# Setup of a long-convolution and feed-forward kernel: layers in quarters, another order of work, stores awaited in the next stage

## The chip, the cores and the metric

The kernel runs on one core of a Trainium2 chip. The metric is the time of one execution on the device, in microseconds (us). A core has TensorE (PE), VectorE (DVE), ScalarE (ACT), GpSimd (POOL) and SyncE (SP), each with its own instruction stream; SP here only issues DMAs and waits. The streams are ordered against each other by semaphores alone.

## The reference, cut to what matters

```python
xn = layernorm(x)                               # x: (4, 2048, 256)
# attention part: two orders of (long convolution, gate)
proj = xn @ in_proj_w + in_proj_b               # 256 -> 768
v = proj[..., :256]
for i in range(2):
    t = linspace(0, 1, 2048)
    ang = 2 * pi * freqs[i] * t
    enc = concat([sin(ang), cos(ang), t])       # 7 features
    h = gelu(enc @ w1[i] + b1[i])               # 64 wide
    h = gelu(h @ w2[i] + b2[i])
    h = (h @ w3[i] + b3[i]) * exp(-abs(decay[i]) * t * 2048)   # 2048 x 256
    v = fft_conv(v, h)
    xc = conv3(proj[..., (i+1)*256:(i+2)*256]) + conv_b[i]
    v = v * xc * sigmoid(xc @ gate_w[i] + gate_b[i])
a = v @ out_proj_w + out_proj_b
# feed-forward part, w_fc (1024 x 256) and w_proj (256 x 1024) made ternary
tern = clip(round(w / s), -1, 1),  s = mean(abs(w), axis=1)
f = relu(xn @ (tern_fc * s).T + gate * (xn @ v_.T @ fast_b.T @ u.T)) ** 2 @ (tern_proj * s_).T
out = x + a + f
```

## The kernel before

The program has three stages, each a block of five streams, with a barrier between two blocks. **Setup** (`setup_stage`) computes from the weights what the others need. **Project** (`project_stage`) goes over 16 chunks of 512 tokens: layer norm, input projection, short convolution, gates. **Mix** (`mix_stage`) does the long convolutions as products with Toeplitz tiles that are read from the DRAM tensor `filters`, the feed-forward part and the output. Only setup and one line of project are touched.

Within a stage every stream is written out by hand, in a fixed order. In setup:

- **The filters.** VectorE makes the time row `t` and the angles, ScalarE their sine into `enc` (L327). TensorE computes layer 1 (L364), ScalarE the gelu over all 2048 columns (L336), TensorE layer 2 (L368), ScalarE its gelu, TensorE layer 3 (L381) as four tiles w = 0 to 3 of 128 channels by 2048 lags. ScalarE makes the windows (Exp, L330) into `hT`. `filter_tile(w)` on VectorE multiplies the tile with its window (L281) and reduces the absolute values of two ranges of lags to `peaks`, the middle one of 128 and the far one of 1663 columns (L286). SP stores each tile to `filters`. At the end the peaks are transposed (L404) and reduced to the integers `flag`, which tell the mix stage how far each filter reaches; a peak counts when it isn't zero.
- **The ternary weights.** `ternary` on VectorE makes `fc_tern` and `pr_tern` from `fc_nat` and `pr_nat` (row means L253, comparisons L258 and L261). TensorE transposes them (L389, L395), ScalarE copies the results out (L348, L350), SP stores them as `fc_t` and `proj_t`. The scales of `w_proj` become a row by way of `diag` (L298, L400).
- **The low-rank part.** M1 is the small product of `v` and `fast_b` (L357); it waits for the four rank loads (`us`, `vs`, `fbT`, `gcol`). `ustack` holds u divided by the fc scales, is transposed (L372) and stored as `u_t`; `vrank` is stored as `v_t`.
- **Projection weights.** `Win` and `Wgate` are split in a high part (ScalarE) and the rest (VectorE, L293, L294).
- **x.** `statistics` on VectorE (L431, L434) and `rstd` and `normalise` on GpSimd prepare the first chunk of tokens.

SP issues all loads in one order, and at the end of setup waits for all 13 counted stores (L54 is the block's end). The project stage's first work on TensorE is the transposition of the first chunk (L795). V and GC1 of the later stages lie over setup's buffers: `hT`, `fc_nat` and the others are parts of V (written first at L651), `t`, `enc`, `h1`, `h2` and `projT` parts of GC1.

## Time and profile before

| | us |
|---|---|
| median of 3 runs | 929.61 |
| the three runs | 923.80, 929.61, 930.54 |
| profiled execution, its own time | 922.28 |
| its span, first to last instruction | 920.4 |
| PE busy | 838.2 (91%) |
| DVE busy | 632.2 (69%) |
| ACT busy | 467.5 (51%) |
| POOL busy | 242.6 (26%) |

The profiled execution is a fourth one beside the three timed runs. Its granted TensorE clock was 0.977 in the mean. Shares are over the whole span; the stages differ much in what they wait for.

### The profile page before, as it was taken

The page shows a single profiled execution, that of the slowest core. Times are in us where ns is not written, and L with a number is a line of the kernel's source. Part 1 is how long each engine was busy: PE and PEld are TensorE (multiplying, and loading weights), DVE is VectorE, ACT ScalarE, POOL GpSimd, SP SyncE. Part 2 cuts the span into 40 slices and gives each one's busy share as a digit, 9 for nine tenths or more (in the row PEclk, how much of TensorE's full clock was granted, in tenths as well). Part 3 has the DMA queues.
Part 4 walks back from the last instruction along what each step waited for, and adds up shares of the span by engine and source line. Part 5 has one row for each costly group of instructions (what it writes and reads, how often), then busy time and mean ns, then how long its engine had stood idle before and what let it go on. Part 6 is the DMA issues. An engine that isn't in the chain of part 4 may idle for free.

```text
span 920.4 us, 25865 instructions
## 1 busy us (share of the span) xinstructions
PE 838.2 (91%) x9894; PEld 699.6 (76%) x9895; DVE 632.2 (69%) x1041; ACT 467.5 (51%) x678; POOL 242.6 (26%) x259
## 2 busy tenths in 40 slices
PE   3837999999999994899999999999999999999995
PEld 1325888888888883678888888788877888788995
DVE  6963799899899885455556555665655556666884
ACT  6422777777777874344444344444434444443221
POOL 1023564664664610201111121210112011210111
PEclk9977999999999998999999999999999999999998
DMA  5363223324324217776787878867787867962893
GB/s 176 116 210 131 100 92 136 138 91 147 127 91 159 93 70 205 188 166 138 167 191 158 174 150 188 188 156 175 140 193 170 184 127 165 202 112 69 232 333 124
DMA packets 84390, 142.02 MB, mean 154 GB/s; under 512 B 12837, under 2 KB 62390, under 8 KB 83318
## 3 DMA queue, kind: packets, MB, share of 16 engines
q1 hardware_dynamic: 73734, 102.79, 47.3%
q0 software_dynamic: 10320, 37.49, 12.7%
q10 hardware_dynamic: 288, 1.11, 0.4%
q8 instruction: 29, 0.48, 0.2%
q14 instruction: 19, 0.16, 0.1%
HBM read 97.39 MB, written 43.97 MB: 154 GB/s over the span
## 4 chain that ended last, share of the span: by engine, by line
PE 43%; DMA 8%; DVE 5%; issue 2%; ACT 1%; SPq 1%; POOL 0%; DVEq 0%; ACTq 0%; POOLq 0%
PE py L1262 12%; PE pp L1243 11%; PE pf L1215 10%; DMA lead<-filters 7%; PE pf L1221 2%; PE py L1299 2%; PE py L1230 2%; DVE r_lo L1060 1%; PE pp L417 1%; PE pp L419 1%; PE pp L418 1%; DVE r L1055 1%; DVE pp L1045 1%; DMA srow<-scales 1%; DVE xb L1050 1%
## 5 line engine op out<-in xcount | busy, mean ns | idle before, releaser
L1262 PEld LDWEIGHTS py<-vwin,lead 64*64 64x64 f32 x5120 | 133.4, 133 | 33.1 <-issue 33.1
L1262 PE MATMUL py<-vwin,lead 64*64 64x128 f32 (+4 forms) x5120 | 147.2, 265 | 8.1 <-DMA lead<-filters 7.4
L1161 ACT ACTIVATE r_hi<-r 128x512 fp32r<-128x512 f32 x128 | 80.9, 632 | 142.9 <-DVE r L1055 142.9
L1060 DVE TENSOR_TENSOR r_lo<-r,r_hi 128x512 fp32r<-128x512 f32 x128 | 103.3, 807 | 67.1 <-ACT r_hi L1161 67.0
L1156 ACT ACTIVATE r<-pf,fscale 128x512 f32<-128x512 f32 x128 | 88.0, 687 | 117.1 <-PE pf L1221 116.9
L1243 PE MATMUL pp<-wproj,r_hi 128*128 128x256 f32 x512 | 134.7, 296 | 8.3 <-DVE r_lo L1060 3.1
L1215 PE MATMUL pf<-tokens,split_a 128*128 (+1 forms) x512 | 139.5, 394 | 0.5 <-issue 0.5
L1243 PE MATMUL pp<-wproj,r_lo 128*128 128x256 f32 x512 | 126.8, 281 | 0.0
L458 POOL TENSOR_SCALAR lead<-lead,norms 128x256 f32<-128x256 f32 x64 | 114.0, 1792 | 3.4 <-POOL norms L452 3.4
L1243 PEld LDWEIGHTS pp<-wproj,r_hi 128*128 128x128 f32 x512 | 96.2, 188 | 21.3 <-issue 6.3
L618 DVE SCALAR_TENSOR_TENSOR xc<-ctrl,taps,xc 128x512 f32<-128x512 f32 x128 | 97.2, 779 | 18.8 <-ACT xc L690 18.1
L1243 PEld LDWEIGHTS pp<-wproj,r_lo 128*128 128x128 f32 x512 | 96.3, 188 | 3.8 <-issue 1.8
L1215 PEld LDWEIGHTS pf<-tokens,split_a 128*128 128x128 f32 x512 | 87.3, 188 | 12.4 <-issue 0.8
L1055 DVE TENSOR_TENSOR r<-r 128x512 f32<-128x512 f32 x128 | 93.4, 730 | 2.0 <-ACT r L1156 1.8
L1399 POOL DMA_DIRECT2D tokens<-xnT_hbm x32 | 17.7, 555 | 180.6 <-PE pf L1221 146.6
L1100 DVE TENSOR_TENSOR V<-py,GC 128x512 f32 (+1 forms) x32 | 22.1, 691 | 61.5 <-PE pp L1243 59.6
L1102 DVE COPY V<-py 128x512 f32 (+1 forms) x32 | 22.1, 691 | 59.4 <-PE pp L1243 59.4
L417 PE MATMUL pc<-tokens,wgate_hi 128*128 128x512 f32 x128 | 54.5, 426 | 7.4 <-DVE tokens L624 7.3
L770 PEld LDWEIGHTS pn<-lead,xnT 128*64 128x64 f32 x1024 | 55.6, 137 | 5.6 <-issue 5.6
L417 PE MATMUL pc<-split_b,split_a 128*128 128x512 f32 x128 | 53.5, 418 | 6.9 <-DVE split_b L662 6.9
L770 PE MATMUL pn<-lead,xnT 128*64 128x128 f32 x1024 | 59.4, 274 | 0.0
L690 ACT ACTIVATE xc<-ctrl,taps 128x512 f32<-128x512 f32 x64 | 51.9, 811 | 13.5 <-DVE ctrl L612 10.3
(175 smaller groups left out, 1535.2 us busy)
## 6 DMA issues: line engine op xcount, KB each, us to landing
lead<-filters SPq DMA_DIRECT2D x128, 320.0 KB, 6.2
xnT_hbm<-split_b SPq DMA_DIRECT2D x32, 512.0 KB, 3.2
tokens<-xnT_hbm POOLq DMA_DIRECT2D x32, 512.0 KB, 7.4
lead<-in_attn_x SPq DMA_DIRECT2D x16, 512.0 KB, 3.9
gc_hbm<-xc SPq DMA_DIRECT2D x16, 512.0 KB, 2.6
GC<-gc_hbm SPq DMA_DIRECT2D x32, 256.0 KB, 7.1
out<-GC POOLq DMA_DIRECT2D x16, 512.0 KB, 5.8
GC<-in_attn_x POOLq DMA_DIRECT2D x9, 512.0 KB, 11.1
```

The costliest lines, as they stand in the source:

```text
L417: pe.matmul(out, w[0], x[0], start=start, stop=False, **more)
L458: last = pool.tensor_scalar(buf[:, i, :], buf[:, i, :], mv[:, i, 0:1], rs[:, i:i + 1], ALU.subtract, ALU.mult)
L618: dve.scalar_tensor_tensor(out=mixed(c), in0=tapped(ctrl[1 - par], c, k_), scalar=kw[:, c, k_:k_ + 1], in1=mixed(c), op0=ALU.mult, op1=ALU ...
L690: act.activation(mixed(c), tapped(ctrl[1 - par], c, 0), ACT.Identity, bias=kb[:, c:c + 1], scale=kw[:, c, 0:1]).then_inc(tap0_done, 1)
L770: last = pe.matmul(pn[side * BW:(side + 1) * BW, i, :].rearrange("p (h c) -> p h c", h=KT), xnT[:, k, ts], Wv_sides[:, k, :, side, :], sta ...
L1055: dve.tensor_tensor(r[j][:, :], r[j][:, :], r[j][:, :], ALU.mult).then_inc(sq_done, 1)
L1060: dve.tensor_tensor(r_lo[j][:, :], r[j][:, :], r_hi[j][:, :].bitcast(F32), ALU.subtract).then_inc(r_split, 1)
L1156: act.activation(r[j][:, :], pf[:, j, :], ACT.Relu, scale=fscale[:, m:m + 1]).then_inc(relu_done, 1)
L1161: act.activation(r_hi[j][:, :], r[j][:, :], ACT.Copy).then_inc(r_hi_done, 1)
L1215: last = pe.matmul(pf[:, m % 2, :], tern[:, k, ws], tokens(even, part, k), start=(k == part == 0), stop=False)
L1243: last = pe.matmul(pp[:, i, :], part[m % 2][:, i * P:(i + 1) * P], wproj[:, m, :], start=(m == 0 and n == 0 and i % 2 == 0), stop=(m == HT ...
L1262: last = pe.matmul(py[g % 2][q * BW:(q + 1) * BW, side, l, :, A:NB], tile[rows, q * PAIR + l, j * BW:(j + 1) * BW], vwin[g % 2][rows, q, l ...
```

## The change

- **Loads.** ScalarE's queue issues `fc_nat`, `vs`, `fbT`, `gcol`, `pr_nat`, `us` first of all; SP issues the loads of the layers, then x, then the rest. Four semaphores (frequencies, layer 1, other layers, each matrix) take the place of coarser ones.
- **Front.** VectorE makes `t` in one instruction, the angles in two halves, ScalarE the sine in two halves. TensorE multiplies two products of `ones` with a buffer of zeros (`warm`) ahead of M1 and two behind it. `enc` and `w1s` get 128 rows, with zeros in the new ones, which GpSimd and VectorE write.
- **Layers** 1 and 2 and their gelus go by quarters of 512 columns, each with its own count. All four windows come behind the gelus.
- **VectorE's order:** thresholds and ternary matrix of fc, statistics of x, tiles 0 and 1, `ustack`, tiles 2 and 3, thresholds of `w_proj`, `diag`, its ternary matrix, scale row, peaks. `filter_tile` reduces only the middle range; ScalarE sums the absolute values of the far one (`far_sum`). GpSimd makes the low parts of `Win` and `Wgate`.
- **Stores.** Setup's SP waits for four small stores alone (pads, `v_t`, `scales`). The other nine are waited for by VectorE in the first step of the project stage, in front of its write to V.

```diff
--- before.py
+++ after.py
...
+        enc = Gf[:, 2 * L:3 * L]
...
+        w1s = sb("w1s", [P, ORDERS * FO])
...
-            load(us[:, :, :], u.rearrange("(m p) r -> p m r", p=P), rank_in)
-            load(vs[:, :], v, rank_in)
-            load(fbT[:, :], fast_b.rearrange("i j -> j i"), rank_in)
-            load(gcol[:, :], bass.AP(gate.tensor, 0, [[0, P], [1, 1]]), rank_in)
...
-            load(fc_nat, w_fc.rearrange("(m p) d -> p m d", p=P), tern_in)
-            load(pr_nat, w_proj.rearrange("(k p) h -> p k h", p=P), tern_in)
...
+            load_x(sp)
...
-            load_first(sp)
+            load_taps(sp)
...
+            sp.wait_ge(ustack_ready, 2)
+            load(v_t, vrank[:, :, :, :].bitcast(F32), small_stored)
+            sp.wait_ge(ternT_ready, 1)
+            load(fc_t, tern.bitcast(F32), stored)
+            sp.wait_ge(srow_ready, 1)
+            load(scales, srow[0:1, :], small_stored)
             sp.wait_ge(ranks_ready, 1)
             load(u_t, ranks.bitcast(F32), stored)
-            sp.wait_ge(ustack_ready, 2)
-            load(v_t, vrank[:, :, :, :].bitcast(F32), stored)
-            sp.wait_ge(ternT_ready, 1)
-            load(fc_t, tern.bitcast(F32), stored)
             sp.wait_ge(proj_ready, 1)
             load(proj_t, projT.rearrange("p (m d) -> p m d", m=HT), stored)
-            sp.wait_ge(srow_ready, 1)
-            load(scales, srow[0:1, :], stored)
-            sp.wait_ge(stored, 16 * 13)
+            sp.wait_ge(small_stored, 16 * 4)
             sp.wait_ge(proj_in, 16 * PROJ_LOADS)
...
             normalise(pool, 0, 0)
+            pool.wait_ge(hi_ready, 1)
+            pool.tensor_tensor(Win[1][:, :, :], win_f[:, :, :], Win[0][:, :, :].bitcast(F32), ALU.subtract)
+            pool.wait_ge(hi_ready, 2)
+            pool.tensor_tensor(Wgate[1][:, :, :], gw_f[:, :, :], Wgate[0][:, :, :].bitcast(F32), ALU.subtract)
...
+            dve.memset(ones[:, :], 1.0).then_inc(warm_ready, 1)
+            dve.memset(warm, 0.0).then_inc(warm_ready, 1)
...
+            for h in range(2):
+                cols = slice(h * L // 2, (h + 1) * L // 2)
+                link(dve.tensor_scalar(rnd[:, cols], turns[:, cols], ROUND, None, ALU.add))
+                dve.scalar_tensor_tensor(out=turns[:, cols], in0=rnd[:, cols], scalar=ROUND, in1=turns[:, cols],
+                                         op0=ALU.subtract, op1=ALU.subtract).then_inc(angle_ready, 1)
...
-                for i, (first, end) in enumerate(((MID_FROM, FAR_FROM), (FAR_FROM, L))):
-                    part = hT[:, w, L - end:L - first] if w < KT else hT[:, w, first:end]
-                    dve.tensor_reduce(peaks[:, i, w:w + 1], part, AX.X, ALU.max, apply_absolute_value=True).then_inc(peak_ready, 1)
-
-            ternary(pr_nat, pr_tern, psc, pth, KT, HID).then_inc(tern_ready, 1)
+                part = hT[:, w, L - FAR_FROM:L - MID_FROM] if w < KT else hT[:, w, MID_FROM:FAR_FROM]
+                dve.tensor_reduce(peaks[:, 0, w:w + 1], part, AX.X, ALU.max, apply_absolute_value=True).then_inc(peak_ready, 1)
+
+            dve.wait_ge(fc_in, 16)
+            thresholds(fc_nat, fsc, fth, HT, D)
+            ternary(fc_nat, fc_tern, fth, HT)
+            statistics(dve, 0, 0, True)
...
-            dve.wait_ge(hi_ready, 2)
-            dve.tensor_tensor(Win[1][:, :, :], win_f[:, :, :], Win[0][:, :, :].bitcast(F32), ALU.subtract)
-            dve.tensor_tensor(Wgate[1][:, :, :], gw_f[:, :, :], Wgate[0][:, :, :].bitcast(F32), ALU.subtract)
...
             filter_tile(2)
+            filter_tile(3)
+            dve.wait_ge(down_in, 16)
+            thresholds(pr_nat, psc, pth, KT, HID)
...
-            filter_tile(3)
-
-            statistics(dve, 0, 0, True)
-
+            ternary(pr_nat, pr_tern, pth, KT)
...
+            act.dma_start(fc_nat, w_fc.rearrange("(m p) d -> p m d", p=P)).then_inc(fc_in, 16)
+            act.dma_start(vs[:, :], v).then_inc(rank_in, 16)
+            act.dma_start(fbT[:, :], fast_b.rearrange("i j -> j i")).then_inc(rank_in, 16)
+            act.dma_start(gcol[:, :], bass.AP(gate.tensor, 0, [[0, P], [1, 1]])).then_inc(rank_in, 16)
+            act.dma_start(pr_nat, w_proj.rearrange("(k p) h -> p k h", p=P)).then_inc(down_in, 16)
+            act.dma_start(us[:, :, :], u.rearrange("(m p) r -> p m r", p=P)).then_inc(rank_in, 16)
...
+                act.wait_ge(angle_ready, h + 1)
+                act.activation(enc[0:TIME_ROW, cols], enc[0:TIME_ROW, cols], ACT.Sin, scale=-TWO_PI).then_inc(enc_ready, 1)
...
+            for j in range(4):
+                act.wait_ge(l1_mm, j + 1)
+                act.activation(h1[:, j * 512:j * 512 + 512], ps[:, j, :], ACT.Gelu, bias=b1s[:, :]).then_inc(h1_ready, 1)
+            for j in range(4):
+                act.wait_ge(l2_mm, j + 1)
+                act.activation(h2[:, j * 512:j * 512 + 512], ps[:, j, :], ACT.Gelu, bias=b2s[:, :]).then_inc(h2_ready, 1)
+
+            act.wait_ge(ndec_ready, 1)
+            for w in range(4):
...
+                act.activation(junk[:, w, 0:L - FAR_FROM], part, ACT.Abs, accum_out=peaks[:, 1, w:w + 1]).then_inc(peak_ready, 1)
+
+            far_sum(0)
+            far_sum(1)
+            act.wait_ge(ternT_mm, 1)
+            act.activation(tern, upper, ACT.Copy).then_inc(ternT_ready, 1)
+            far_sum(2)
+            far_sum(3)
...
+            pe.wait_ge(warm_ready, 2)
+            for _ in range(2):
+                pe.matmul(ps[:, 7, :], ones[:, :], warm, start=True, stop=True)
             pe.wait_ge(rank_in, 16 * RANK_LOADS)
-            pe.wait_ge(ident_ready, 1)
...
+            for _ in range(2):
+                pe.matmul(ps[:, 7, :], ones[:, :], warm, start=True, stop=True)
+
+            pe.wait_ge(layer1_in, 16 * LAYER1_LOADS)
+            pe.wait_ge(t_row_ready, 1)
+            for j in range(4):
+                pe.wait_ge(enc_ready, j // 2 + 1)
+                pe.matmul(ps[:, j, :], w1s[:, :], enc[:, j * 512:j * 512 + 512], start=True, stop=True).then_inc(l1_mm, 1)
...
-            pe.wait_ge(h1_ready, 1)
-            for j in range(4):
-                last = pe.matmul(ps[:, j, :], w2s[:, :], h1[:, j * 512:j * 512 + 512], start=True, stop=True)
-            last.then_inc(l2_mm, 1)
-            pe.wait_ge(ustack_ready, 2)
-            for m in range(HT):
-                last = pe.transpose(upper[0:HALF, m * P:(m + 1) * P], ustack[:, m, :, :].bitcast(F32).rearrange("p s r -> p (s r)"), ident[:, :])
-            last.then_inc(uT_mm, 1)
-            pe.wait_ge(h2_ready, 1)
-            pe.wait_ge(ranks_ready, 1)
+                pe.wait_ge(h1_ready, j + 1)
+                pe.matmul(ps[:, j, :], w2s[:, :], h1[:, j * 512:j * 512 + 512], start=True, stop=True).then_inc(l2_mm, 1)
+            pe.wait_ge(ustack_ready, 1)
...
+                    if w == 0:
+                        pe.wait_ge(h2_ready, j + 1)
...
+            pe.wait_ge(ustack_ready, 2)
+            pe.wait_ge(ternT_ready, 1)
+            for m in range(HT):
+                last = pe.transpose(upper[0:HALF, m * P:(m + 1) * P], ustack[:, m, :, :].bitcast(F32).rearrange("p s r -> p (s r)"), ident[:, :])
+            last.then_inc(uT_mm, 1)
+            pe.wait_ge(diag_ready, 1)
+            pe.matmul(ps[:, 6, 0:D], ones[:, :], diag[:, :, :].rearrange("p k c -> p (k c)"), start=True, stop=True).then_inc(srow_mm, 1)
...
                     dve.wait_ge(v_mm, s + 1)
+                    if s0 == 0:
+                        dve.wait_ge(stored, 16 * STORES)
```

TensorE's order in setup, from its first product to layer 3 (GC1 holds `enc`, `h1` and `h2`; a row with x3 is three more of its kind). Before:

```order
L357 MATMUL ps_setup<-fbT,vs 128x16 [waits ident_ready,rank_in]
L364 MATMUL ps_setup<-GC1,w1s 128x512 [waits enc_ready,t_row_ready,filter_in]
L364 MATMUL ps_setup<-GC1,w1s 128x512 x3
L368 MATMUL ps_setup<-GC1,w2s 128x512 [waits h1_ready]
L368 MATMUL ps_setup<-GC1,w2s 128x512 x3
L372 MATMUL ps_setup<-ident,GC1 64x128 [waits ustack_ready]
L372 MATMUL ps_setup<-ident,GC1 64x128 x7
L381 MATMUL ps_setup<-GC1,w3s 128x512 [waits ranks_ready,h2_ready]
```

After (V is the part that holds `warm`):

```order
L380 MATMUL ps_setup<-V,ones 128x512 [waits warm_ready]
L383 MATMUL ps_setup<-fbT,vs 128x16 [waits rank_in]
L386 MATMUL ps_setup<-V,ones 128x512 x2
L392 MATMUL ps_setup<-GC1,w1s 128x512 [waits enc_ready,t_row_ready,layer1_in]
L392 MATMUL ps_setup<-GC1,w1s 128x512 [waits enc_ready] x3
L396 MATMUL ps_setup<-GC1,w2s 128x512 [waits h1_ready,filter_in]
L396 MATMUL ps_setup<-GC1,w2s 128x512 [waits h1_ready] x3
L405 MATMUL ps_setup<-GC1,w3s 128x512 [waits h2_ready,ustack_ready]
L405 MATMUL ps_setup<-GC1,w3s 128x512 [waits h2_ready] x3
```

Four products are new, every quarter waits for its own input, and the transposes of `ustack` (L372) have left this place.

VectorE's order from the first filter tile to the scale row. Before:

```order
L281 SCALAR_TENSOR_TENSOR V<-ps_setup,b3s,V 128x2048 [waits l3_mm,win_ready]
L286 TENSOR_REDUCE peaks<-V 128x1 [waits h_ready]
L286 TENSOR_REDUCE peaks<-V 128x1
L293 TENSOR_TENSOR split_a<-win_f,split_a 128x1024 [waits hi_ready]
L294 TENSOR_TENSOR wgate_lo<-gw_f,wgate_hi 128x1024
L298 TENSOR_SCALAR diag<-ident,psc 128x128 [waits ident_ready]
L431 BN_STATS norms<-lead 128x6 [waits x_loaded0]
L305 TENSOR_TENSOR peaks<-peaks 128x4 [waits peak_ready]
L307 COPY scale_row<-ps_setup 128x256 [waits srow_mm]
```

After, from the last filter tile on:

```order
L283 SCALAR_TENSOR_TENSOR V<-ps_setup,b3s,V 128x2048 [waits l3_mm,win_ready]
L287 TENSOR_REDUCE peaks<-V 128x1 [waits h_ready]
L273 TENSOR_REDUCE psc<-V 128x2 [waits down_nat_in]
L306 TENSOR_SCALAR diag<-ident,psc 128x128 [waits ident_ready,dve_step]
L265 TENSOR_SCALAR V<-V,pth 128x1024 x2
L268 SCALAR_TENSOR_TENSOR V<-V,pth 128x1024 [waits dve_step]
L311 COPY scale_row<-ps_setup 128x256 [waits srow_mm]
L313 TENSOR_TENSOR peaks<-peaks 128x4 [waits peak_ready]
```

The second ternary matrix (its reduction L273, comparisons L265 and L268) stands behind the tiles instead of ahead of them; the statistics and the low parts are gone from there.

## Rows read from the trace of the kernel before

**Rows 1.** windows view: us, busy us of PE, PEld, DVE, ACT, POOL; clock, DMA, GB/s

```profile
0.00:67.90 67.90, 35.98 (x102) 18.03 (x103) 51.24 (x84) 29.13 (x20) 10.35 (x20) 0.93 0.57 170
```

**Rows 2.** the waits of SP's queue, 0 to 110 us; total, times, longest

```profile
SPq L54 <- DMA scales<-scale_row: 4.9, 1, 4.9
```

**Rows 3.** the block end L54, 60 to 70 us; duration min/median/max in ns

```profile
L54 POOLq DRAIN  x1: 4837/4837/4837, 61.3 to 61.3; - x1
```

**Rows 4.** timeline of TensorE, 0 to 110 us; start, us, what, [idle before]

```profile
6.67 1.03 PE L357 MATMUL ps_setup<-fbT,vs 16*128 16x16 f32 x4 [6.67 <-DMA gcol<-in_ffn_gate]
14.52 7.16 PE L364 MATMUL ps_setup<-GC,w1s 65*128 65x512 f32 x8 [6.82 <-ACT GC L327]
23.74 5.80 PE L368 MATMUL ps_setup<-GC,w2s 128*128 128x512 f32 x8 [2.06 <-ACT GC L336]
...
32.59 14.25 PE L381 MATMUL ps_setup<-GC,w3s 128*128 128x512 f32 x32 [2.18 <-ACT tokens L343]
...
54.65 3.03 PE L395 MATMUL ps_setup<-ident,V 128*128 128x128 f32 x16 [2.89 <-DVE V L281]
...
58.35 1.21 PE L404 MATMUL ps_setup<-ident,peaks 128*1 128x128 f32 x8
67.98 1.94 PE L795 MATMUL pT<-ident,lead 128*128 128x128 f32 x8 [8.42 <-PEq L54]
```

**Rows 5.** timeline of TensorE's weight loads, 21 to 31 us

```profile
27.32 0.34 PEld L368 LDWEIGHTS ps_setup<-GC,w2s 128*128 128x128 f32 x1 [0.52 <-issue]
28.09 0.19 PEld L368 LDWEIGHTS ps_setup<-GC,w2s 128*128 128x128 f32 x1 [0.44 <-issue]
```

**Rows 6.** timeline of ScalarE, 0 to 110 us

```profile
14.39 1.28 ACT L330 ACT_TABLE_LOAD   x1
15.69 3.89 ACT L330 ACTIVATE V<-GC,ndec 128x2048 f32<-128x2048 f32 x2
...
21.72 1.97 ACT L336 ACTIVATE GC<-ps_setup,b1s 128x2048 f32<-128x2048 f32 x1 [0.84 <-PE ps_setup L364]
```

**Rows 7.** timeline of VectorE, 0 to 110 us

```profile
19.09 2.29 DVE L253 TENSOR_REDUCE fscale<-V 128x8 f32<-128x2048 f32 x1 [6.17 <-DMA V<-in_ffn_w_proj]
...
28.68 2.27 DVE L253 TENSOR_REDUCE psc<-V 128x2 f32<-128x2048 f32 x1
...
32.91 2.48 DVE L261 SCALAR_TENSOR_TENSOR V<-V,pth 128x1024 f32<-128x1024 f32 x2
36.37 2.35 DVE L281 SCALAR_TENSOR_TENSOR V<-ps_setup,b3s,V 128x2048 f32<-128x2048 f32 x1 [0.98 <-PE ps_setup L381]
...
51.77 0.47 DVE L298 TENSOR_SCALAR diag<-ident,psc 128x128 f32<-128x128 f32 x2
52.15 2.35 DVE L281 SCALAR_TENSOR_TENSOR V<-ps_setup,b3s,V 128x2048 f32<-128x2048 f32 x1
...
59.60 0.68 DVE L310 TENSOR_REDUCE reach<-ps_setup 1x1 f32<-1x512 f32 x1 [0.61 <-PE ps_setup L404]
...
61.85 0.18 DVE L316 CAST flag<-reach 1x65 int32<-1x65 f32 x1
...
85.49 1.23 DVE L651 TENSOR_TENSOR V<-pn,bv_row 128x1024 f32<-128x1024 f32 x1 [2.84 <-PE pn L770]
```

**Rows 8.** VectorE's groups by line and form, 19 to 62 us

```profile
L286 DVE TENSOR_REDUCE peaks<-V 128x1 f32<-128x1663 f32 x4 | 7.5, 1874 | 0.0
```

**Rows 9.** timeline of SP's queue, 0 to 110 us

```profile
10.43 0.59 SPq L137 DMA_DIRECT2D V<-in_ffn_w_fc  x1
...
61.45 0.81 SPq L137 DMA_DIRECT2D scales<-scale_row  x1
```

**Rows 10.** DMA issues, 0 to 75 us; KB each, median us to landing

```profile
V<-in_ffn_w_proj SPq DMA_DIRECT2D x1, 1024.0 KB, 8.0
...
us<-in_ffn_u SPq DMA_DIRECT2D x1, 64.0 KB, 2.3
```

**Rows 11.** GpSimd's groups by line and form, whole span

```profile
L984 POOL TENSOR_TENSOR xb<-xb,bo_row 128x1024 f32<-128x1024 f32 x7 | 17.8, 2536 | 45.3 <-DMA xb<-in_attn_x 45.3
```

149 lines of the change are left out of this document (71 added, 78 removed).

## Prediction

> **What bounds the kernel now.** I read the views in this order. The windows view puts the whole setup stage into 0 to 67.9 us [rows 1]. In it TensorE works 36.0 us of 67.9, VectorE 51.2, ScalarE 29.1: no engine is full, so setup is a chain that changes engines, and the change touches nothing else. Behind it the project and mix stages stay as they are; they start from a barrier, so setup's end moves them as a block, and what counts is when TensorE's first product of the project stage (L795) starts, now at 67.98 [rows 4].
>
> Three things end late. VectorE writes the flags until 62.03 (61.85 + 0.18) [rows 7]. GpSimd, which gets the statistics of x last, leaves its drain at 66.1 (61.3 + 4.84) [rows 3]. SP issues the last store at 61.45, is free at 62.26 and waits 4.9 us for the stores to land, until 67.16 [rows 2, 9]; TensorE starts 0.8 us later.
>
> The chain to 62.03, backwards [rows 4, 7]: the last filter tile is multiplied by VectorE from 52.15; the four tiles start at 36.37, when L381 has filled the first banks. L381 (layer 3) starts at 32.59, and is ready for it only because layer 1 starts at 14.52 (waiting for the sine), layer 2 at 23.74 and each gelu takes a whole 2048 columns (1.97 us, [rows 6]) between layers. VectorE's own load is the other strand: it waits for both weight matrices until 19.09, and makes both ternary matrices before tile 0.
>
> **The change part by part.** Times are on the clock of the profiled execution.
>
> *TensorE's front.* Layer 1 will be behind the small product M1 and two pairs of products of zeros. The trace counts each full fp32 product as two passes: eight for four products. At the lower clock a pass costs 7.16/8 = 0.895 us, at the higher 14.25/32 = 0.445 [rows 4]. Pair one runs from about 2.5 to 6.1 while nothing else could. M1 waits for all four rank loads, and `us` is now last on ScalarE's queue, behind both weight matrices. Before, the two matrices took from 10.43 (issue) to 19.09 (VectorE starts on them), 8.6 us [rows 7, 9]. Issued from about 1.0 they are in at 9.7. `us` alone took 2.3 us from issue to landing [rows 10]; issued by 4, it is in the same queue right behind, so I add 0.8 us for its bytes: 10.5, with bounds of 8 (it does not wait for the matrices' ends) and 13 (SP's x loads take half of the engines from 8 us on). Before, M1 started at 6.67: this part of the change costs a wait. M1 takes 1.03 [rows 4], ends at 11.5; pair two, 4 x 0.895 = 3.6, ends at 15.1. So layer 1 starts 0.6 us *later* than now, at 15.1. The sine is no bound any more: it was ready at 14.52, and loses a conversion and one of VectorE's passes and is cut in halves.
>
> *The clock.* The eight passes of layer 1, with 65 rows, keep TensorE busy for 7.16 us at 0.895 each and the clock does not rise; the passes of layer 2, with 128 rows, start slow at 23.74 and the weight load at 28.09 is the first short one (0.19 instead of 0.34 us), 4.35 us later [rows 4, 5]. That is the step from 1.2 to 2.4 GHz. The change gives layer 1 128 rows and puts 128-row products ahead. Taking 4.35 us from 11.5, the clock is up at 15.9: layer 1 pays one slow pass and seven fast, 0.9 + 3.1, and ends at 19.1. Bounds: clock up already at 15.1 (0.4 us less), or only when layer 1 is done (7 x 0.45 = 3.2 us more).
> The Trainium skill ("TensorE: Matmul & The Clock Gate", Part 1) says that the default is the slow clock and sustained activity releases it. Layer 1's 7.16 busy us at the slow rate say that busy time alone is not enough here; by the page layer 1 would be fast from its first pass, 0.4 us less, by the row as summed.
>
> *Quarters.* Layer 2's pass over quarter j waits for gelu j alone. A quarter of a gelu is about 0.5 to 0.7 us (1.97 for four, [rows 6]), less than the 0.89 of a quarter's two passes, so TensorE runs through: layer 2 19.1 to 22.7, layer 3's first tile right behind. The present gaps of 2.06 and 2.18 us ahead of layers 2 and 3, and the eight transposes of `ustack` between them, are gone from there. Layer 3 keeps its 14.25 us [rows 4]: 22.7 to 37.0. The windows (Exp) now come after the gelus: last gelu at about 23.4, one table load of 1.28, 1.95 for each [rows 6]: the first at 26.6, tile 0's products at 26.3. So VectorE starts tile 0 at 26.7 instead of 36.37, and each tile (2.35 + a short reduction) is quicker than TensorE's 3.56 for the next. The long reductions of 1.87 us, four of them [rows 8], go to ScalarE, where there is room: windows until 32.5, two copies, four sums of about 1.6 (1663 columns at the gelu's rate), two more copies, some 44 in all, before the 46.9 below. VectorE reaches tile 0 with time left: it is held until M1's result at about 12.3, then comes the first ternary matrix, which with the `ustack` steps took from 19.09 to 28.68, 9.6 us [rows 7]; that leaves 4.8 us ahead of 26.7 for the four short statistics instructions.
>
> Tile 3 starts at **37.1 instead of 52.15: 15.0 us earlier**.
>
> *The tail gets longer.* The second ternary matrix moves behind tile 3. It took from 28.68 to 35.39 (32.91 + 2.48), 6.7 us, the diagonal 0.47 [rows 7]. 37.1 + 2.35 + 0.3 + 6.7 + 0.5 = 46.95. Only then can TensorE transpose it, 3.03 us at the low clock, and the peaks, 1.21 [rows 4]: 51.2. The flags' chain was 59.60 to 62.03, 2.4 us [rows 7]; with 0.2 of hand-over it ends at **53.8, 8.2 us earlier than 62.03**. The statistics of x are done by 26.7, so GpSimd normalises long before; the two low parts of weights that it takes over (about 2.5 us each by its nearest row, [rows 11]) end near 41.
>
> *The stores.* SP now waits only for four small ones. The 4.9 us go, and with them the 5.1 us from 62.03 to 67.16. Behind the tail nothing waits: barrier and start 0.8 us as before, 54.6. **67.98 - 54.6 = 13.4 us.** The wait is moved in front of VectorE's first write to V, which was at 85.49 [rows 7] and will be at 72.1. The last large store, issued at 46.95 + 3.0 + 1.9 (ScalarE's copy, a 2048-column instruction) + 0.5 = 52.4, lands some 5.7 us later (61.45 to 67.16 with two large ones in the queue [rows 2, 9]): 58.1, so 14 us of cover. Without this cover the 5.1 us would come back, no more.
> The Trainium skill ("DMA: Bandwidth & Descriptors", Issuing engines are not separate DMA queues) speaks against the second queue: transfers from all queues run on the same engines, and only issue time is saved. Here issue order is what held the matrices back (fc was issued at 10.43); by that rule the sharing with x puts M1 at the upper bound, 13, which gives a gain of 10.9 instead of 13.4.
>
> **From the gain to a time.** The profiled execution took 922.28 us with a span of 920.4; less 13.4 it is 908.9. It is the fastest of the four times known: the median of the runs is 929.61, less 13.4 it is 916.2. I take the middle of the four (923.8 and 929.61, mean 926.7): **913.3 us**, a ratio of 1.015. A measurement of this kernel can tell about 1% (9 us) from no change.
>
> **Rivals.**
> (a) *Late front.* `us` lands at 13, or the clock rises only behind layer 1. For: the queue is in order, and SP loads x at the same time. Against: the two matrices alone were done in 8.6 us. It costs 2.5 to 5.7 us: gain 7.7 to 10.9, time about 917.5. Chance 0.20, about half of it above 1%.
> (b) *The clock stays low: slower than before.* If products of zeros and the broken stream do not raise TensorE (7.16 us of layer 1 did not), every pass of the layers costs 0.45 us more: 7 + 8 + 32 passes, 21.2 us, against 13.4 gained: 7.8 us slower, 934.5. It decides from 30 slow passes on. Against: layer 2 rose after 4.35 us with 128 rows, and after 15.1 the new order has no gap. Chance 0.04.
> (c) *Early front.* `us` in at 8, clock up when layer 1 starts: 3 us more, gain 16 to 17, time 910. Chance 0.10.
> (d) *The tail is fuller than I see*, or the change does not remove the wait at the end: stores still queued hold one of SP's small ones (the scales are behind the transposed fc matrix). If SP again waits 5 us, gain 8.3: 918.4. Against: the scales are issued near 47.5, 6 us before VectorE's end. Chance 0.08, with other losses that leave under 1%, or a small loss, 0.06 more.
> The forecast itself, gain 11 to 16: 0.52.
>
> **Numbers.** Faster by over 1%: the forecast, (c), half of (a), a part of (d), some of it lost where runs scatter: 0.74. Slower by over 1%: 0.05. Within 1%: 0.21. The range takes the gains from 8 to 17 on the scatter of the base: 905 to 922.
>
> **What will show it.** In the changed profile: M1 near 10.5 and layer 1 near 15; short weight loads from about 16; L283's four tiles from 26.7 to 37; L55 without a DMA wait on SP; the first pT transposes at 54.6; V written near 72 without idle time put down to a store. If M1 starts much later than 10.5, step *TensorE's front* is wrong; if L392 to L405 have passes of 0.85, *the clock*; if L827 starts more than 1 us after VectorE's flag cast, *the stores*. The prediction fails as a whole if the project or mix stage changes its own length, 852.4 us from 67.98 to the end.

## Result and the profile after

The changed kernel takes 917.07 us (four runs, 913.4 to 923.1) against 927.83 us for the one before (four runs, 923.8 to 930.5): a ratio of 0.9876, 95% interval 0.984 to 0.9912, or 10.8 us. A second set on another occasion gave 915.54 us (six runs) against 927.22 us (eleven), again 0.9876 [0.9846, 0.9906], 11.7 us. The forecast was 913.3 us in a range of 905 to 922.

The profiled execution took 916.67 us, with a span of 915.1 us. TensorE's timeline in setup shows the start, the layers, the tail and the hand-over to the project stage, against [rows 4] (start, us, what, idle before it and its releaser):

```profile
2.68 3.78 PE L380 MATMUL ps_setup<-V,ones 128*128 128x512 f32 x4 [2.68 <-DVE V L234]
11.92 1.03 PE L383 MATMUL ps_setup<-fbT,vs 16*128 16x16 f32 x4 [5.46 <-DMA us<-in_ffn_u]
12.88 3.78 PE L386 MATMUL ps_setup<-V,ones 128*128 128x512 f32 x4
16.45 4.40 PE L392 MATMUL ps_setup<-GC,w1s 128*128 128x512 f32 x8
20.69 3.60 PE L396 MATMUL ps_setup<-GC,w2s 128*128 128x512 f32 x8
24.12 13.90 PE L405 MATMUL ps_setup<-GC,w3s 128*128 128x512 f32 x32
...
47.88 3.67 PE L427 MATMUL ps_setup<-ident,V 128*128 128x128 f32 x16 [2.62 <-DVE V L268]
51.34 1.46 PE L434 MATMUL ps_setup<-ident,peaks 128*1 128x128 f32 x8
55.88 1.94 PE L827 MATMUL pT<-ident,lead 128*128 128x128 f32 x8 [3.08 <-PEq L55]
```

The first transpose of the project stage is at 55.88 instead of 67.98 us: **setup is 12.1 us shorter**. This start is the measure of all setup experiments below. It is steadier than the time of a run, but not exact: two more profiles with this same setup have it at 55.71 and 54.59, and the kernel before has it at 67.98 and 68.31. So the gain of setup is 12.1 to 13.7 us by the pair that is compared, and a difference of 1.3 us or less at this point shows nothing by itself. The start of tile 3 on VectorE (38.13, 38.37 and 37.29 in the three) leaves the tail's part of this scatter out. Between layers 1, 2 and 3 there is no idle time in brackets any more, where [rows 4] had 2.06 and 2.18 us; on the other side stands a new wait of 5.46 us for `us`. The weight loads show the rise of the clock at 18.12, as [rows 5] do at 28.09:

```profile
17.31 0.34 PEld L392 LDWEIGHTS ps_setup<-GC,w1s 128*128 128x128 f32 x1 [0.52 <-issue]
18.12 0.19 PEld L392 LDWEIGHTS ps_setup<-GC,w1s 128*128 128x128 f32 x1 [0.47 <-issue]
```

VectorE's timeline, against [rows 7]: tile 0, tile 3, the ternary form of `w_proj` behind it, the flags, and the first write to V, which now follows the wait for the stores:

```profile
28.36 2.35 DVE L283 SCALAR_TENSOR_TENSOR V<-ps_setup,b3s,V 128x2048 f32<-128x2048 f32 x1 [4.08 <-ACT V L355]
...
38.13 2.35 DVE L283 SCALAR_TENSOR_TENSOR V<-ps_setup,b3s,V 128x2048 f32<-128x2048 f32 x1 [0.38 <-PE ps_setup L405]
...
40.72 2.27 DVE L273 TENSOR_REDUCE psc<-V 128x2 f32<-128x2048 f32 x1
...
45.34 2.48 DVE L268 SCALAR_TENSOR_TENSOR V<-V,pth 128x1024 f32<-128x1024 f32 x2
...
52.84 0.68 DVE L316 TENSOR_REDUCE reach<-ps_setup 1x1 f32<-1x512 f32 x1 [4.61 <-PE ps_setup L434]
...
55.09 0.18 DVE L322 CAST flag<-reach 1x65 int32<-1x65 f32 x1
...
72.80 1.22 DVE L683 TENSOR_TENSOR V<-pn,bv_row 128x1024 f32<-128x1024 f32 x1 [2.84 <-PE pn L802]
```

Two readings matter here. The flag cast ends at 55.27 and TensorE starts 0.6 us later, so no store is waited for at the end of setup. And V's first write waits 2.84 us for TensorE, to the hundredth what it waited before [rows 7]: the deferred wait for nine stores costs nothing there. SP's queue confirms the end: the last store is issued before VectorE is done, and of the 4.9 us wait for a DMA of [rows 2] there is nothing.

```profile
48.18 0.24 SPq L143 DMA_DIRECT2D scales<-scale_row  x1
48.46 0.48 SPq L143 DMA_DIRECT2D u_t<-tokens  x1
53.49 0.33 SPq L143 DMA_DIRECT2D proj_t<-GC  x1
```

From the first transpose to the end the two profiled executions differ the other way: 852.4 us before, 859.2 us after. That pair alone would say that half of the gain is handed back. The last part of the next section is about it.

### The profile page after: what moved, and what is told of

It reads as the page before. It is cut to its first block, busy times and chain, and to the rows that moved or that the text cites. A ratio compares the mean times of both kernels' runs of the same rounds, so it can differ in the third digit from the quotient of the medians.

```text
span 915.1 us, 25896 instructions
## 1 busy us (share of the span) xinstructions
PE 842.4 (92%) x9902; PEld 701.7 (77%) x9903; DVE 625.7 (68%) x1036; ACT 472.7 (52%) x692; POOL 247.6 (27%) x262
## 4 chain that ended last, share of the span: by engine, by line
PE 44%; DMA 6%; DVE 6%; issue 3%; ACT 1%; SPq 0%; DVEq 0%; POOL 0%; ACTq 0%; POOLq 0%
PE py L1294 12%; PE pp L1275 12%; PE pf L1247 10%; DMA lead<-filters 5%; PE pf L1253 2%; PE py L1331 2%; PE py L1262 2%; DVE r L1087 1%; DVE r_lo L1092 1%; DVE pp L1077 1%; PE pp L447 1%; PE pp L449 1%; PE pp L448 1%; DVE xb L1082 1%; DMA srow<-scales 1%
## 5 line engine op out<-in xcount | busy, mean ns | idle before, releaser
L1092 DVE TENSOR_TENSOR r_lo<-r,r_hi 128x512 fp32r<-128x512 f32 x128 | 105.5, 825 | 67.1 <-ACT r_hi L1193 67.0
L722 ACT ACTIVATE xc<-ctrl,taps 128x512 f32<-128x512 f32 x64 | 51.9, 811 | 13.7 <-DVE ctrl L642 10.5
## 6 DMA issues: line engine op xcount, KB each, us to landing
GC<-in_attn_x POOLq DMA_DIRECT2D x9, 512.0 KB, 11.9
```

Source lines behind the costliest of these rows:

```text
L722: act.activation(mixed(c), tapped(ctrl[1 - par], c, 0), ACT.Identity, bias=kb[:, c:c + 1], scale=kw[:, c, 0:1]).then_inc(tap0_done, 1)
L1092: dve.tensor_tensor(r_lo[j][:, :], r[j][:, :], r_hi[j][:, :].bitcast(F32), ALU.subtract).then_inc(r_split, 1)
```

## Experiments

Each starts from the changed kernel unless it says otherwise. Its own first transpose is compared with 55.88 us.

### The stores are waited for in setup again

```diff
             sp.wait_ge(small_stored, 16 * 4)
+            sp.wait_ge(stored, 16 * STORES)
```

> The changed kernel, but SyncE waits in setup for all 13 stores again, as before the change. Measured by the start of projection's first transpose in the profile (55.88 us in the changed kernel). Theory, from the profile of the changed kernel: proj_t is issued at 53.49 and has landed at about 57.4, VectorE's last instruction ends at 55.27, so the block would end 2.1 us later, and the first transpose stands at 58.0 to 58.5: the deferred stores were worth 2 to 2.5 us of the 12.1. Rival: SyncE is 4 to 5 us late, as in the kernel before, where its last wait ended beside a drain of GpSimd of 4.8 us: first transpose at 60 to 61.

First transpose at 58.63. The layers and tile 3 were 0.35 us late in this run (tile 3 at 38.48 against 38.13), which leaves 2.4 us; and from the end of the flag cast (55.78) to the first transpose it is 2.85 us instead of 0.61. So the deferred stores are worth 2.2 to 2.4 us. The waits of SP's queue name the one that is back:

```profile
SPq L143 <- ACT GC L375: 4.5, 1, 4.5
SPq L199 <- DMA proj_t<-GC: 3.5, 1, 3.5
```

The rival falls: not 5 us, since only one store is still under way when VectorE ends, and VectorE ends 2 us behind the issue of that store.

### TensorE without products of zeros, with 65 rows, and with neither

```diff
-            for _ in range(2):
-                pe.matmul(ps[:, 7, :], ones[:, :], warm, start=True, stop=True)
```
in both places for the first, for the second
```diff
-                pe.matmul(ps[:, j, :], w1s[:, :], enc[:, j * 512:j * 512 + 512], start=True, stop=True).then_inc(l1_mm, 1)
+                pe.matmul(ps[:, j, :], w1s[0:TIME_ROW + 1, :], enc[0:TIME_ROW + 1, j * 512:j * 512 + 512], start=True, stop=True).then_inc(l1_mm, 1)
```
and both edits for the third.

> The changed kernel without its four products of zeros (two ahead of M1, two behind it); layer 1 still runs over 128 rows. Theory: layer 1 then starts where the first sine ends (12.95 us, against 16.45), its first passes run slow and the clock rises some 4 to 5 us after it starts, at 17 to 18, as it does now; layer 1 ends at 19 to 20 (20.85 now), and tile 3 and the setup's end come 0 to 1.5 us earlier: the products of zeros cost what they give. Rival, the way the change is written: without them TensorE is at half clock through layer 2, the gelus of layer 2 end 1 us or more later than the 25.0 of now, and projection's first transpose comes 1 to 3 us later than 55.88.

> The changed kernel, but layer 1 multiplies 65 rows as before instead of 128 (63 of them zeros). Theory: the clock rises by the share of TensorE's rows in use, so the 65-row passes leave it low; all eight passes of layer 1 and the first of layer 2 are slow, with short weight loads (0.19 us) appearing only 2 us or more later than 18.12; the second gelus end 1 to 3 us later than 25.0, and the setup ends 1 to 3 us later. Rival: busy time alone raises the clock, whatever the rows: weight loads become short at 18.1 +- 0.4, and nothing moves by over 0.4 us.

> The changed kernel with no products of zeros and layer 1 over 65 rows: neither of the two edits that were to raise the clock. Without the zero products alone the clock rose 4.4 us after layer 1 began (128 rows, from 12.97), and layer 1 ended at 18.9; with 65 rows but the zero products it had risen at 16.35. Theory: in passes of 65 rows the clock does not rise, as in the kernel before (8 passes, 7.16 us, all slow): layer 1 ends at 19.8 to 20.2, layer 2 stays slow for 3 to 4 us, layer 3 begins 1 to 2.5 us later than in the run without zero products alone (21.76), and projection's first transpose comes at 55.5 to 57, against 54.58. Rival: the rows do not matter: clock up at 17.4, first transpose at 54.2 to 55.0.

| kernel | layer 1 starts | first short weight load | layer 1 takes | layer 3's first load | tile 3 starts | first transpose |
|---|---|---|---|---|---|---|
| changed | 16.45 | 18.12 | 4.40 | 23.70 | 38.13 | 55.88 |
| changed, second profile | 17.21 | 17.93 | 3.88 | 23.94 | 38.37 | 55.71 |
| changed setup in the run without bias, below | 16.42 | 16.42 | 3.60 | 22.86 | 37.29 | 54.59 |
| no zero products | 12.97 | 17.89 | 5.94 | 21.76 | 36.19 | 54.58 |
| 65 rows | 16.35 | 16.35 | 3.60 | 22.79 | 37.23 | 54.58 |
| neither | 13.94 | 23.41 | 7.20 | 25.13 | 39.56 | 57.53 |

The windows view cannot tell the level of the clock this early: it reads 1.00 for the eight slow passes of before (14.52 to 21.70), because the trace's first record of the clock is its rise, at 28.0. Ahead of that, the length of a pass tells it: 0.90 us at the low clock, 0.45 at the high one.

Without the zero products tile 3 starts 1.1 to 2.2 us *earlier* than in the three profiles of the changed setup (1.1 to 2.1 with M1 at the same time): layer 1 waits for the second pair, and without it the clock rises during layer 1 itself. At the first transpose only 0.0 to 1.3 us of this are seen, since VectorE waited longer for the peaks (5.07 us against 4.15 to 4.61). With 65 rows alone nothing is lost, against my theory: the clock had risen at the end of the second pair, and all eight 65-row passes behind it are fast. It rose early in this run, 3.4 us after that pair began instead of 5.2. That is no work of the edit, and neither are the 1.3 us of this row: the run without bias has the changed setup with all 128 rows, and shows the same early rise and the same end, to 0.1 us:

```profile
16.42 3.60 PE L392 MATMUL ps_setup<-GC,w1s 128*128 128x512 f32 x8
...
54.59 1.94 PE L827 MATMUL pT<-ident,lead 128*128 128x128 f32 x8 [3.08 <-PEq L55]
```

What passes over 65 rows did in no profile is raise the clock from the low level. That shows where neither edit is there:

```profile
13.94 7.20 PE L388 MATMUL ps_setup<-GC,w1s 65*128 65x512 f32 x8
20.93 4.79 PE L392 MATMUL ps_setup<-GC,w2s 128*128 128x512 f32 x8
```

All eight passes of layer 1 are slow again, 7.20 us as in [rows 4] (7.16), without a gap, and weight loads get short at 23.41, 3.3 us after those of layer 2 with 128 rows began (20.08). In this run `us` landed about 1 us late; less that, tile 3 would be at about 38.6 and the first transpose at about 56.6. So, without zero products, 128 rows in layer 1 are worth some 2.4 us at tile 3 and 2.0 at the first transpose (each from one profile). At tile 3 the zero products take back 1.1 to 2.1 of these 2.4, and the clock part of the change nets 0.3 to 1.3 us.

### The load of `us` first

```diff
+            act.dma_start(us[:, :, :], u.rearrange("(m p) r -> p m r", p=P)).then_inc(rank_in, 16)
             act.dma_start(fc_nat, w_fc.rearrange("(m p) d -> p m d", p=P)).then_inc(fc_in, 16)
...
-            act.dma_start(us[:, :, :], u.rearrange("(m p) r -> p m r", p=P)).then_inc(rank_in, 16)
```

> The changed kernel, but the load of u (the fourth that M1 waits for) is issued first on ScalarE's queue instead of behind both weight matrices; M1 waited 5.46 us for it. Theory: M1 runs at 7 to 8.5 us instead of 11.9; the second pair of zero products follows it and is over before the sine (12.05); layer 1 starts at 12.1 to 13.0 instead of 16.45 and the tiles and the end of setup come 1.5 to 4 us earlier. If TensorE falls idle between the zero products and the sine, layer 1 runs slow for 4 to 5 us from its start and the gain is nearer 1.5. Rival: M1 is late for another load (v, fast_b or the gate, all issued on the same queue), then nothing moves by over 0.5 us.

First transpose at 51.64: **3.0 to 4.2 us earlier** than in the three profiles of the changed setup (tile 3, at 34.35, 2.9 to 4.0 us), the largest gain that a single edit added to the changed kernel. Its timeline:

```profile
9.02 0.61 PE L383 MATMUL ps_setup<-fbT,vs 16*128 16x16 f32 x4 [2.56 <-DMA gcol<-in_ffn_gate]
9.56 3.46 PE L386 MATMUL ps_setup<-V,ones 128*128 128x512 f32 x4
12.82 3.86 PE L392 MATMUL ps_setup<-GC,w1s 128*128 128x512 f32 x8
```

`us` lands 2.4 us after its issue, not 7.8; what is now late is the gate, which is still issued behind the first matrix, so M1 comes at 9.02 and not at 7 to 8.5. The clock rises in the first passes of layer 1 (weight loads of 0.19 us from 13.51), and VectorE goes from the statistics into tile 0 at 24.70 without its wait of 4.08 us.

### The ternary form of `w_proj` ahead of tile 0

```diff
             statistics(dve, 0, 0, True)
+            dve.wait_ge(down_in, 16)
+            thresholds(pr_nat, psc, pth, KT, HID)
+            ternary(pr_nat, pr_tern, pth, KT)
             filter_tile(0)
```
(and out from behind tile 3)

> The changed kernel, but VectorE makes the ternary form of w_proj (8 instructions, 6.7 us) behind the statistics of x, ahead of tile 0, where it waited 4.08 us for ScalarE's window, and not behind tile 3. Theory: VectorE is 2.6 us late for tile 0 and the four tiles shift by that; behind tile 3 there are 6.7 us less of VectorE's work; projT's transposes then follow tile 3 directly, and projection's first transpose comes 3.5 to 4.5 us earlier than 55.88, at 51.4 to 52.4. Rival: the tail is bound by TensorE and ScalarE (transposes, the copies of tern and ranks), and the shift of 2.6 us eats what is left: 0 to 1.5 us earlier, or later.

First transpose at 55.36: 0.5 us earlier than 55.88 and 0.8 later than 54.59, so no gain is shown, the rival's case. Tile 0 came at 30.69, as forecast, but the way to tile 2 grew, and the tail was bound elsewhere:

```profile
33.08 8.83 PE L405 MATMUL ps_setup<-GC,w3s 128*128 128x512 f32 x16 [2.69 <-DVE V L283]
42.02 1.94 PE L414 MATMUL ps_setup<-ident,V 128*128 128x128 f32 x16
46.02 1.13 PE L419 MATMUL ps_setup<-ident,GC 128*64 128x128 f32 x8 [2.06 <-ACT tokens L368]
```

TensorE's transposes of fc wait until VectorE has read tile 2 out of the same banks (41.87), and from there the chain is transposes, ScalarE's copy, transposes of `ustack`, transposes of projT, whoever made the ternary matrix. VectorE's copy of `ustack` stands in the way too, 2.47 us instead of 0.43; its row, and the one of GpSimd beside it:

```profile
36.82 2.47 DVE L301 CAST GC<-GC 128x512 fp32r<-128x512 f32 x1
```
```profile
36.60 2.40 POOL L219 TENSOR_TENSOR wgate_lo<-gw_f,wgate_hi 128x1024 fp32r<-128x1024 f32 x1
```

It ends (39.29) just behind GpSimd's two-input instruction (39.00), and in the changed kernel, where GpSimd's begins at 35.04, it runs ahead of it at 0.43.

### The far parts by VectorE again

```diff
                 dve.tensor_reduce(peaks[:, 0, w:w + 1], part, AX.X, ALU.max, apply_absolute_value=True).then_inc(peak_ready, 1)
+                far = hT[:, w, 0:L - FAR_FROM] if w < KT else hT[:, w, FAR_FROM:L]
+                dve.tensor_reduce(peaks[:, 1, w:w + 1], far, AX.X, ALU.max, apply_absolute_value=True).then_inc(peak_ready, 1)
...
-            far_sum(0)
-            far_sum(1)
...
-            far_sum(2)
-            far_sum(3)
```

> The changed kernel, but VectorE reduces the far part of each filter tile to its peak again (four reductions of 1663 elements, 1.87 us each) and ScalarE's four far sums are gone. Theory: VectorE is the busy engine from tile 0 to the end of w_proj's ternary form (waits of 0.23 and 0.38 us in 20 us), so nearly all of the 7.5 us comes back: projection's first transpose at 62 to 63.5 us instead of 55.88. Rival: the tail is bound by the transposes and ScalarE's copies as much as by VectorE, and only 2 to 4 us come back (58 to 60).

First transpose at 66.04, 10.2 us later; less 1.4 us for an M1 at 13.33, **8.8 us** (10.1 against the profile at 54.59), beyond the theory's 7.5 for the four instructions themselves. The rest are their followers: the same copy of `ustack` beside GpSimd (2.45 us), and TensorE, idle for 4.01 us ahead of the transposes, which then take 3.65 instead of 1.91 us, at the low clock:

```profile
44.16 3.65 PE L412 MATMUL ps_setup<-ident,V 128*128 128x128 f32 x16 [4.01 <-DVE V L283]
```

Of the parts tried, moving the far sums is worth most: without it the rest of the change would be worth some 3 us (67.98 against 64.6).

### Gelus in halves

```diff
-            for j in range(4):
-                act.wait_ge(l1_mm, j + 1)
-                act.activation(h1[:, j * 512:j * 512 + 512], ps[:, j, :], ACT.Gelu, bias=b1s[:, :]).then_inc(h1_ready, 1)
+            for j in range(2):
+                act.wait_ge(l1_mm, 2 * j + 2)
+                act.activation(h1[:, j * 1024:j * 1024 + 1024], lower[:, j * 1024:j * 1024 + 1024], ACT.Gelu, bias=b1s[:, :]).then_inc(h1_ready, 1)
```
and layer 2's alike.

> The changed kernel, but the gelus of both layers run in halves of 1024 columns (four ScalarE instructions instead of eight), and layers 2 and 3 wait for halves. Theory: quarters hide all of ScalarE's latency in TensorE's layers; with halves layer 2 starts where it does now or 0.3 us later, the last gelu of layer 2 ends 0.3 to 1.0 us later than 25.0, and all that follows is 0.3 to 1.5 us later than 55.88. Rival, the way the forecast counted it: with halves TensorE waits 2 us ahead of layer 2 and again ahead of layer 3, as in the kernel before, its clock falls, and the first transpose is 3 us or more later.

First transpose at 55.77. TensorE runs through the three layers all the same (16.63, 20.68, 24.12), since half a gelu (1.11 us) is shorter than the four passes it hides behind (1.72). Tile 0 came 0.4 us later and tile 3 0.3 us later than in the changed kernel; at the first transpose nothing of it can be told from the scatter. The rival falls: no wait and no slow clock come back with halves. That cutting the layers at all is what matters is read from [rows 4] (2.06 and 2.18 us of waiting ahead of layers 2 and 3, which are gone); no run has the changed kernel with uncut layers.

### GpSimd's additions in the mix stage

The profile after shows instructions of VectorE in the mix stage that take 1.8 to 2.9 us instead of 0.69, each beside an addition of GpSimd (a row of GpSimd's timeline, then one of VectorE's):

```profile
728.26 2.39 POOL L1016 TENSOR_TENSOR GC<-GC,bo_row 128x1024 f32 x1 [9.11 <-DMA GC<-in_attn_x]
```
```profile
728.49 2.70 DVE L1092 TENSOR_TENSOR r_lo<-r,r_hi 128x512 fp32r<-128x512 f32 x1 [0.70 <-ACT r_hi L1193]
```

GpSimd's ends at 730.65 and VectorE's half a microsecond later, at 731.19. What these instructions take beyond 0.69 us sums to 24.6 us after (14 of them) and to 20.9 before (13).

```diff
-                pool.tensor_tensor(buf, buf, bo_row[:, :].unsqueeze(1).broadcast_to([P, TT, D]), ALU.add).then_inc(xb_biased, 1)
+                pool.tensor_tensor(buf[:, 0, 0:1], buf[:, 0, 0:1], bo_row[:, 0:1], ALU.add).then_inc(xb_biased, 1)
```

> The changed kernel without the addition of out_proj's bias to x in the mix stage: GpSimd adds one element instead of 128x1024 (its output lacks that bias). In the changed kernel's profile 14 of GpSimd's 16 additions (2.4 us each) ran beside a two-input instruction of VectorE, which then took 2.1 to 2.9 us instead of 0.69, 24.6 us in all. Theory: with the additions gone no VectorE instruction of r or r_lo takes over 0.9 us there; TensorE waits less for r_lo, the kernel is 5 to 20 us shorter than 917, and its runs lie within 2 us of one another. Rival: the collisions lie beside TensorE's work: under 3 us, and the runs scatter as before by 7 us or more.

> The kernel before, with the same addition left out. Theory: without the collisions' scatter the two kernels differ by what setup gained less what is given back: 12.1 us less 2.5 us for GpSimd's drain at the start of mix (9.57 against 7.05 us), so this run is 9 to 12 us longer than the changed kernel without bias. Rival: the collisions themselves took part of the gain (their sum was 20.9 us before, 24.6 after), and then the difference grows to 12 to 14 us.

912.83 us (six runs, 909.7 to 919.1) and 924.01 us (twelve, 919.9 to 927.0), beside 928.18 us (seventeen, 921.7 to 932.1) for the kernel before. The hits are gone from both, which the group of L1092 of the changed kernel without bias shows (mean 689 ns, against 825 in the changed kernel):

```profile
L1092 DVE TENSOR_TENSOR r_lo<-r,r_hi 128x512 fp32r<-128x512 f32 x128 | 88.2, 689 | 67.1 <-ACT r_hi L1193 67.0
```

But 20.9 us of VectorE are worth only about 4 us of the kernel before (ratio 0.9963 [0.9941, 0.9985]) and 24.6 us only 3 to 4 of the changed one (between its two medians and 912.83), and the runs scatter over 7 to 9 us as before. The hits are real and mostly hidden; the scatter is not theirs. The two kernels differ by 11.2 us here, where their first transposes differ by 13.7 (68.31 and 54.59).

### Where the runs scatter, and a combined version

```diff
+            pe.wait_ge(ranks_ready, 1)
+            pe.wait_ge(peak_ready, 9)
+            for i in range(2):
+                for w in range(4):
+                    last = pe.transpose(ps[0:1, 4 + i, w * P:(w + 1) * P], peaks[:, i, w:w + 1], ident[:, :])
+            last.then_inc(peakT_mm, 1)
             pe.wait_ge(tern_ready, 2)
             pe.wait_ge(h_ready, 4)
```
The combined version has `us` first as well, and VectorE's maximum of the peaks stands between the two halves of the ternary form.

> The changed kernel with u's load issued first on ScalarE's queue, and with the transposes of the peaks (and VectorE's maximum ahead of them) moved in front of the transposes of projT, so that VectorE's reach chain of 2.4 us runs beside projT's copy. With u first alone the first transpose came at 51.64. Theory: the peaks are transposed at 42.0, VectorE ends at 46.9 and the end is set by ScalarE's copy of projT at 49.6 and the issue of its store: first transpose at 50.1 to 50.8, 5.1 to 5.8 us earlier than 55.88, and the median of runs 4 to 6 us under that of the changed kernel. Rival: VectorE waits for ScalarE's far sums inside the ternary form, projT comes later by that, and nothing is gained over 51.64.

> The changed kernel once more, unchanged, for a second profile and a time on the same chip as the combined version. Theory: first transpose at 55.3 to 56.8 (the load of u and the rise of the clock each scatter by half a microsecond or more), median 915 to 918; its time from there on is 855 to 862 us like that of the other runs, longer than the 852.4 of the profiled execution of the kernel before only because that one was 6 us faster than its median. Rival: the rest is always 857 or more after the change and the kernel before has 852, so that half of setup's gain is handed back; then the medians would differ by 6 us.

The combined version starts projecting at 50.20, 5.7 us earlier than the changed kernel's first profile and 4.4 earlier than its earliest. Its flags are cast by 46.48, and the end is now ScalarE's copy of projT (48.98) and the store's issue. Its median is 908.94 us (905.3 to 917.0), a ratio to the kernel before of 0.9805 [0.9765, 0.9845], 6.6 us under the changed kernel on the same chip.

The changed kernel once more has its first transpose at 55.71 and again 859.2 us from there on. Over all profiles that rest is 852.4 us (before) and 853.2 (before without bias); after, it is 854.7, 856.8, 857.9, 858.4, 858.9, 859.2, 859.2, 859.5, 860.8, 861.5, 861.6 and 866.8. The profiled execution of before is 5.9 us faster than the median of its 17 runs; a median run of it has a rest of 858.3 if its setup is the same, and a median run of the changed kernel has 858.1 to 859.6. From medians the setup's 12.1 us arrive as 10.8 and 11.7, so 0.4 to 1.3 us are given back, no more than these medians can tell; against a setup that is 13.7 us shorter it would be 2.0 to 2.9, and the kernels without bias say 2.5. Of the 6.8 us between the first two profiles 4.6 lie in the mix stage (from TensorE's first product there to the end 551.0 us before and 555.7 after; 552.0 before without bias, 551.4 to 564.0 over all profiles after). Both profiles of before have a shorter rest than all twelve after, though most of these are variants. Whether anything of this is real, and where it comes from, stays open. A candidate was the wait of TensorE at the block between project and mix, 6.4 us before and 8.9 after. It does not hold: the kernel before without bias has 8.2 there, and two changed variants 7.3 and 6.3.

A part of the scatter is one wait. At the start of the second order TensorE waits for a filter block; these are the rows of before, of the changed kernel, and of the version with halves, in that order:

```profile
681.05 2.28 PE L1262 MATMUL py<-vwin,lead 64*64 64x128 f32 x80 [1.89 <-DMA lead<-filters]
```
```profile
671.80 2.28 PE L1294 MATMUL py<-vwin,lead 64*64 64x128 f32 x80 [1.92 <-DMA lead<-filters]
```
```profile
677.65 4.28 PE L1294 MATMUL py<-vwin,lead 64*64 64x128 f32 x80 [4.09 <-DMA lead<-filters]
```

After a wait of 1.9 us the 80 products take 2.28 us, after 4.1 us (3.65 with `us` first) 4.28 us, and in the combined version 3.61 us after 2.88: the clock has fallen. At this place the wait is 1.9 to 4.1 us over the fourteen profiles. The four profiles after the change with 3.5 us or more have a rest of 862.0 us in the mean, the other eight one of 858.4; but these eight alone spread from 854.7 to 861.5, so most of the scatter has other causes, which were not looked for. The windows view of that iteration gives both costs together, 33.0 us at a granted clock of 1.00 (the changed kernel again) and 37.9 us at 0.91 (halves):

```profile
660.60:693.60 33.00, 30.76 (x526) 25.63 (x525) 18.15 (x25) 13.18 (x21) 4.64 (x4) 1.00 0.81 166
```
```profile
664.90:702.80 37.90, 33.55 (x526) 28.26 (x525) 16.15 (x25) 13.18 (x21) 4.72 (x4) 0.91 0.72 148
```

A wait that is 2.1 us longer goes with an iteration that is 4.9 us longer. What makes that block late in one run and not in another was not tried.

## Why the prediction was right, and where it was not

The outcome was the forecast's own case by setup's gain: 12.1 us where 13.4 were counted (11 to 16), none of the rivals (b), (c) or (d). The other pairs of profiles give 12.3 to 13.7. The gain in time, 10.8 us, would also fit rival (a), and its mechanism, a late front, is there at part of its price. By its steps:

- *TensorE's front*: M1 10.5 forecast, 11.92 measured (12.68 in the second profile); layer 1 15.1 against 16.45. In direction this was right, down to layer 1 starting later than before the change, and the 0.8 us by which `us` lands behind the matrices was too (1.0). The matrices were late: the sum carried the 8.6 us of before over to an issue at 1.0 and had them in at 9.7, and they landed at 10.85. So `us`, issued at 4.03 behind two loads of 1 MB, needed 7.8 us. This is rival (a)'s mechanism at half of its lower price (1.4 of 2.5 us), and moving one line removes it. What followed from the Trainium skill ("DMA: Bandwidth & Descriptors", Issuing engines are not separate DMA queues) was an M1 at 13, since loads of both queues share the engines; the measured 11.9 to 13.3 (over the ten profiles that kept this order of loads) lie nearer to that than my 10.5.
- *The clock*: rise forecast 4.35 us behind M1's end, at 15.9; it came at 18.12, 5.2 us behind. The same stretch was 4.9 (no zero products), 3.4 (65 rows) and 3.3 (neither), and the kernel before itself has 5.2 in its second profile (the one without bias), so the one row of before was no constant. Forecast was one slow pass in layer 1, there were about two, and layer 2 began at 20.69 and not at 19.1.
- *Quarters*: no gaps between the layers, right; layer 3 took 13.90 us. Tile 0 at 28.36 (forecast 26.7) and tile 3 at 38.13 (37.1): tile 0 waits for ScalarE's window, behind gelus that ended 1.6 us late, and tile 3 for TensorE, 1.4 us late at the start of layer 3 and 0.35 quicker in it. The cut's fineness did not count, as the halves show. Of the 14.0 us by which tile 3 comes earlier (52.15 to 38.13) 6.5 hang on the far parts' move to ScalarE (tile 3 at 46.04 without it, less 1.4 for its late M1), and 8.8 at the hand-over; the prediction did not price this move by itself.
- *The tail gets longer*: from tile 3 to the last flag 16.7 us forecast, 17.14 measured (38.13 to 55.27); the transposes of projT took 3.67 instead of 3.03. Right, and the early-ternary run shows why it could not simply be moved back.
- *The stores*: release 0.6 us (forecast 0.8), first V write at 72.80 (72.1) without a store's wait. Right. But the 4.9 us of [rows 2] were not all to be had from this edit: in the new order the wait is worth 2.2 to 2.4 us.
- *From the gain to a time*: the base of 926.7 was close to the medians of later sets (927.2 to 928.2). Of the miss of 3.8 us (917.07 against 913.3) 1.3 are setup's in the first pair of profiles; the other 2.5 are the base, the rest of the kernel and the scatter of four runs a side, whose interval alone is 8 to 15 us of gain.

The prediction named a change of length in project and mix as what would make it fail as a whole. By that sentence the first pair of profiles says that it failed, 852.4 to 859.2. The test was too sharp for two single profiles: the profiled execution of before was 5.9 us faster than its median, and medians leave 0.4 to 1.3 us. But not all of it is explained so: the profile of before without bias lies near its median (923.44 against 924.01) and has 853.2, where a median run of the changed kernel without bias has 856.5. That the time came out well inside the range rests on this difference being small, which the prediction assumed and did not show.

Not tried one by one are the angles and sine in halves, uncut layers in the new order, and the move of the statistics of x, without which GpSimd's drain (until 66.1 in [rows 3]) might hold the end of setup once the stores are no longer waited for.

## What to carry to other kernels

Measure a change of one stage by that stage's hand-over in the profile: here it scattered by 1.3 us, where the time of a run scattered by 10. Take two or three profiles of the same kernel first, to know that scatter. Before issuing loads from a second queue, list which tiny load the first product waits for and issue that first; a 64 KB load behind two of 1 MB cost 3.0 to 4.2 us here. Filler products that are to raise the clock have to fit into idle time: here the real work waited for them, and they cost 1.1 to 2.1 us at tile 3, while layer 1 over 128 rows raised the clock itself.

## What the hardware showed

- Eight passes over 65 rows ran 7.20 us without a gap, all at the low clock of 1.2 GHz (0.90 us each), and 7.16 and 7.17 us in the two profiles of before; behind 128-row products that had brought the high one, 2.4 GHz, the same eight passes ran in 3.60 us at it (granted clock 1.00), to the last. The Trainium skill ("TensorE: Matmul & The Clock Gate", Part 1) speaks of sustained activity, and the first of these rows is sustained without a rise.
- The same sequence at the start (second pair of zero products, then layer 1 over 128 rows, same loads) saw its next fast weight load 3.2 to 6.0 us after the pair's start in seven profiles (5.2 and 4.3 in two of one and the same kernel). In the mix stage, groups of 80 products that had waited 1.96 and 2.20 us for a filter block were slow in part (3.42 and 3.95 us), one that had waited 2.35 us was fast (2.28), and none that had waited 2.37 us or more was wholly fast.
- A VectorE instruction beside a two-input instruction of GpSimd can last until just behind the end of that one, 0.54 and 0.29 us in the rows shown: 2.70 us for 0.69 (two inputs), and 2.47 for 0.43 (a copy in fp32).
